# Running five of eight experts over gathered token rows in the last mixture of a twelve-stage decoder kernel

## The chip, the cores and the metric

The kernel runs on one core of a Trainium2 chip. The metric is the device time of one execution in microseconds (us). The program is one launch; its stages follow each other with a barrier of all engines between them.

## The reference

`x` is (8 batches, 128 tokens, 128 features), so 1024 tokens in all. Four layers follow, each an attention, a cross attention and a feed-forward part, always as `x = x + part(layernorm(x))`. The change concerns the last part, a mixture of eight experts with two experts a token and a capacity of 320 places an expert:

```python
cap = floor(2 * 1.25 * 1024 / 8)             # 320
logits = xt @ w_g                            # (1024, 8)
top_v, top_i = top_k(logits, 2)
probs = softmax(logits with all but the two at -inf)
exp_mask = one_hot(top_i, 8) by choice       # first choices of all tokens, then second choices
exp_rank = cumsum(exp_mask over 2 * 1024) - 1
exp_mask = exp_mask * (exp_rank < cap)       # a token whose rank is 320 or more is dropped by that expert
exp_batches = tokens of each expert, 320 rows each
h = gelu(exp_batches @ c_fc)                 # 128 -> 512 for each expert
exp_out = h @ c_proj                         # 512 -> 128
out = sum over the two choices of prob * the token's row of exp_out
```

## The kernel before

All arithmetic is float32. The residual `x_res` lies in SBUF as 128 token rows by 8 batches by 128 features; `xn` is its layer norm, `xnT` the same turned so that features are on partitions and the 1024 tokens are columns.

The last stage is `layer_l3_ffn`, which calls `mixture`. Every expert is run over all 1024 tokens, in two halves of 512 columns: 8 experts x 2 halves = 16 units. A unit is an `up` step on TensorE (four matmuls L1016, each 128 hidden features by 512 tokens, into banks 0 to 3), four gelu activations on ScalarE (L1055) into `hT`, a `down` step on TensorE (16 matmuls L1026: four groups of 128 tokens, each summed over four blocks of hidden features, into one of banks 4 to 6), and four VectorE instructions (L1074) that add the result, scaled by the token's gate for this expert (zero where the expert wasn't chosen or the token was dropped), to `x_res`. The order on TensorE is written out: `up(u)`, then `down(u - 1)`.

Ahead of the units, the layer norm (VectorE L413 to L425, one POOL instruction for each half, L439), eight turns on TensorE (L445) and the router's eight matmuls (L888) run. The routing itself, `RouteWithCapacity.dve`, is a chain of small VectorE instructions in which each waits for the one before (`Link`). It ends with `picked`; TensorE then counts ranks with four small matmuls (`pe_counts`, L931 and L933), which stand behind `up(2)` in its order; VectorE then drops ranks of 320 and more (L962) and makes the gates.

SyncE (SP) loads the weights of each expert (L994, L995; 256 KB each), two experts ahead. POOL does nothing in this stage but the two norm instructions, and no DMA is issued from POOL anywhere in this kernel. Behind the stage comes the block "finish": SP stores `x_res` to `out` and waits for it.

The functions that the diff touches, and what calls them:

## Time and profile before

| | us |
|---|---|
| median of 3 runs (lowest, highest) | 1444.35 (1442.29, 1446.95) |
| the profiled execution, its own time | 1439.21 |
| its span, first to last instruction | 1437.4 |
| TensorE busy in the span | 1257.7 |
| VectorE busy | 698.8 |
| ScalarE busy | 527.4 |
| POOL busy | 393.8 |

The rows below come from the profiled execution. A line such as L1026 is a line of the kernel's file. "PE" is TensorE's matmuls, "PEld" its weight loads, "DVE" VectorE, "ACT" ScalarE, "SPq" SP's queue. One float32 matmul of the program stands in the trace as two records, so x32 of L1026 (or x8 of L1016) is one unit's step. The end of a matmul is modelled in the trace; the pace of TensorE is therefore read from the distance between starts, or from the chain that ended last.

### The profile page before, as it was taken

How to read it: one execution, taken by the hardware profiler on the slowest of the kernel's cores; microseconds unless marked ns; L12 is line 12 of the kernel's file. 1: busy time of each engine (PE TensorE's matmuls, PEld its weight loads, DVE VectorE, ACT ScalarE, POOL GpSimd, SP SyncE). 2: the span in 40 equal slices, each digit the busy share in tenths (PEclk: the TensorE clock that was granted, in tenths of full speed). 3: DMA queues.
4: the chain of work that ended last, by engine and by line, in shares of the span. 5: the costliest groups of instructions: out<-in, count | busy, mean ns of one | idle time of the engine just before them, and what ended most of it. 6: DMA issues, size and time to landing. Idle time of an engine off the chain costs nothing. (4 is left out here: it accounts for less than half of the span.)

```text
span 1437.4 us, 26031 instructions
## 1 busy us (share of the span) xinstructions
PE 1257.7 (87%) x10476; PEld 929.3 (65%) x10476; DVE 698.8 (49%) x2173; ACT 527.4 (37%) x1183; POOL 393.8 (27%) x459
## 2 busy tenths in 40 slices
PE   7999697999866766987887999999899999987998
PEld 5867585788623433664664887785567774565776
DVE  5554533444499245764674226527732137655111
ACT  5533242443355323453443212314433324333332
POOL 7959120000423226744662300002000010040000
PEclk9999798999956678998999559999989989988999
DMA  4000503321380000000000000000021100000010
GB/s 138 1 4 1 190 1 103 89 65 26 118 226 1 1 32 0 1 1 1 1 1 8 2 2 1 1 4 1 9 87 39 36 14 1 4 0 30 30 45 30
DMA packets 46695, 48.42 MB, mean 34 GB/s; under 512 B 18960, under 2 KB 37904, under 8 KB 45552
## 3 DMA queue, kind: packets, MB, share of 16 engines
q1 hardware_dynamic: 46576, 46.76, 10.4%
q8 instruction: 84, 1.38, 0.4%
q14 instruction: 35, 0.29, 0.1%
HBM read 41.91 MB, written 4.85 MB: 33 GB/s over the span
## 5 line engine op out<-in xcount | busy, mean ns | idle before, releaser
L1026 PEld LDWEIGHTS bank<-scratch 128*128 128x128 f32 x1024 | 119.0, 192 | 13.9 <-issue 13.9
L1055 ACT ACTIVATE scratch<-bank 128x512 f32<-128x512 f32 x128 | 76.4, 597 | 135.2 <-PE bank L1016 135.2
L1026 PE MATMUL bank<-scratch 128*128 128x128 f32 x1024 | 119.2, 275 | 0.0
L1016 PE MATMUL bank<-xnT,scratch 128*128 128x512 f32 x256 | 118.7, 609 | 0.0
L1074 DVE SCALAR_TENSOR_TENSOR x_res<-bank,scratch,x_res 128x128 f32<-128x128 f32 x128 | 36.0, 345 | 168.0 <-PE bank L1026 168.0
L615 ACT ACTIVATE scratch<-bank 128x512 f32<-128x512 f32 x96 | 52.5, 594 | 91.7 <-PE bank L516 91.7
L574 DVE TENSOR_REDUCE scratch<-bank 128x4 f32<-128x512 f32 x96 | 63.2, 686 | 38.2 <-PE bank L2180 22.4
L1016 PEld LDWEIGHTS bank<-xnT,scratch 128*128 128x128 f32 x256 | 47.9, 197 | 49.1 <-issue 49.1
L439 POOL TENSOR_TENSOR ln_rstd<-ln_ve,ln_half 128x4 f32<-128x4 f32 x28 | 28.6, 1024 | 178.2 <-DVE ln_ve L418 178.1
L2432 POOL TENSOR_TENSOR scratch<-scratch 128x16 f32<-128x16 f32 x16 | 51.7, 3231 | 52.2 <-DVE scratch L2773 52.2
L580 DVE TENSOR_TENSOR scratch<-bank,scratch 128x512 f32<-128x512 f32 x96 | 61.5, 682 | 0.0
L516 PEld LDWEIGHTS bank<-ident,scratch 128*128 128x128 f32 x384 | 43.9, 146 | 23.9 <-DVE scratch L580 17.0
L516 PE MATMUL bank<-ident,scratch 128*128 128x128 f32 x384 | 54.9, 288 | 4.7 <-DVE scratch L580 4.7
L2170 PE MATMUL bank<-weights 32*128 32x32 f32 x1024 | 54.6, 395 | 2.5 <-DVE scratch L2284 2.5
L2170 PEld LDWEIGHTS bank<-weights 32*128 32x128 f32 x1024 | 54.5, 327 | 3.3 <-issue 3.3
L500 PE MATMUL bank<-scratch 32*128 32x512 f32 x192 | 55.2, 656 | 1.4 <-ACT scratch L2253 1.4
L2461 PE MATMUL bank<-weights,xnT 128*128 128x512 f32 x64 | 40.0, 721 | 14.4 <-DVE scratch L2743 13.8
L2135 POOL TENSOR_TENSOR weights<-weights 128x128 f32<-128x128 f32 x8 | 3.7, 457 | 154.3 <-DVE weights L2314 154.3
L2975 POOL TENSOR_TENSOR scratch<-scratch 128x1024 f32<-128x1024 f32 (+5 forms) x48 | 42.9, 893 | 3.8
L445 PE MATMUL bank<-ident,xn 128*128 128x128 f32 x88 | 21.4, 381 | 23.9 <-DVE xn L425 23.8
L1598 POOL TENSOR_TENSOR x_res<-x_res,scratch 128x256 f32<-128x256 f32 x4 | 2.9, 724 | 142.8 <-ACT scratch L1742 142.8
L2970 POOL TENSOR_TENSOR scratch<-scratch 128x2048 f32<-128x2048 f32 x8 | 36.2, 4525 | 19.7 <-DVE weights L1311 19.3
(527 smaller groups left out, 2835.3 us busy)
## 6 DMA issues: line engine op xcount, KB each, us to landing
scratch<-conv_kernels SPq DMA_DIRECT2D x8, 1024.0 KB, 11.2
scratch<-e_l_ffn_w SPq DMA_DIRECT2D x32, 256.0 KB, 2.9
scratch<-e_l_ffn_w SPq DMA_DIRECT2D x4, 1024.0 KB, 14.5
values<-scratch SPq DMA_DIRECT2D x8, 512.0 KB, 2.7
scratch<-values SPq DMA_DIRECT2D x8, 512.0 KB, 4.2
weights<-w_l_ffn SPq DMA_DIRECT2D x1, 3698.0 KB, 12.2
weights<-w_l_attn SPq DMA_DIRECT2D x1, 2560.5 KB, 9.0
weights<-w_l_attn SPq DMA_DIRECT2D x2, 1024.0 KB, 7.1
```

The source lines that it names most:

```text
L500: s = self.nc.tensor.matmul(self.by_head(self.core.ps[n % 4][:, :]), self.qT[rows, b * P:(b + 1) * P], self.km[rows, :, b * P:(b + 1) * P] ...
L516: t = self.nc.tensor.transpose(self.core.ps[4 + n % 2][:, i * P:(i + 1) * P], self.shift[:, n % 4, i * P:(i + 1) * P], self.core.ident[:, :])
L574: self.nc.vector.tensor_reduce(self.top[:, n % 4, :], self.by_head(self.core.ps[n % 4][:, :]), AX_X, ALU.max, negate=True).then_inc(self.t ...
L580: self.nc.vector.tensor_tensor(self.by_head(self.shift[:, n % 4, :]), self.by_head(self.core.ps[n % 4][:, :]), self.top[:, n % 4, :].unsqu ...
L615: self.nc.scalar.activation(self.prob_of(n), self.by_head(self.core.ps[4 + n % 2][:, :]), ACT.Exp, scale=scale) \
L1016: nc.tensor.matmul(ps[UP_BANKS[i]][:, :], wa[e % 2][:, i * P:(i + 1) * P], core.xnT[:, half(h)], start=True, stop=True).then_inc(up_made.s ...
L1026: mm = nc.tensor.matmul(ps[Y_BANKS[u % 3]][:, t * P:(t + 1) * P], hT[h][:, i, t * P:(t + 1) * P], wb[e % 2][:, i, :], start=(i == 0), stop ...
L1055: nc.scalar.activation(hT[u % 2][:, i, :], ps[UP_BANKS[i]][:, :], act_func) \
L2170: m = nc.tensor.matmul(ps[4 * (r % 2) + j][:, 32 * t:32 * t + 32].rearrange("p (i b) -> p i b", i=4), relk[rows, P - 1 - q:2 * P - 1 - q], ...
L2432: nc.gpsimd.tensor_tensor(rn, ss, power, ALU.pow).then_inc(rooted.sem, rooted.up())
L2461: nc.tensor.matmul(ps[QK_BANKS[n]][:, :], core.xnT[:, b * P:(b + 1) * P], wqkv[d][:, n * BANK:(n + 1) * BANK], start=True, stop=True).then ...
L2975: link(tt(out, prod[:, :, 0:h], prod[:, :, h:2 * h], ALU.add))
```

## The change

`layer_l3_ffn` gets a program of its own in place of `mixture`. Experts 0, 1 and 7 are run as before over all tokens in halves (jobs 0 to 3 and 9, 10). Experts 2 to 6 (jobs 4 to 8) are run over 320 columns each. Their token rows are brought together through DRAM:

- The router also computes for each token and choice a row number (`places`): a row of 1600 (5 x 320) if the choice is one of the five experts and not dropped, else an unused row behind them. The counting matmuls now stand behind `down(0)`. The gate normalization, which stood ahead of `picked`, now stands behind it.
- POOL writes the rows of `xn` to DRAM (`rows_of_tokens`) with 16 indirect DMAs, one for each batch and choice, 128 rows of 512 bytes each. When all 16 have landed, SP reads the 1600 rows back in four DMAs as 13 tiles of 128 rows; TensorE turns them (13 transposes in four groups), VectorE copies each group to `takenT`.
- Each of the five jobs is an `up` of four matmuls over 320 columns, four gelus over 320, a `down` of 12 matmuls, two VectorE copies to `made`, and two DMAs of SP into DRAM (`rows_of_experts`).
- When all ten of those have landed, POOL reads each token's row back with 16 indirect DMAs into `back`, and VectorE adds them with their gates to `x_res` in four groups (16 instructions, L1350), behind the additions of expert 7.
- All experts' weights are loaded at the start of the stage, 4 MB in eight DMAs. At the start of the kernel POOL clears a tile of zeros and SP writes it over the 13 tiles of `rows_of_tokens`.

```diff
-class RouteWithCapacity(Route):
+class RouteToPlaces(Route):
...
+    FIRST, LAST = 2, 7
+    ROWS = (LAST - FIRST) * CAP
...
-        dve.wait_ge(self.exped.sem, self.exped.at(0))
-        link(nc.vector.tensor_tensor(prob, prob, second, ALU.mult))
-        link(nc.vector.tensor_reduce(self.total, prob, AX_X, ALU.add))
-        link(nc.vector.reciprocal(self.total, self.total))
-        link(nc.vector.tensor_tensor(prob, prob, over_experts(self.total), ALU.mult))
...
         v.then_inc(self.picked.sem, self.picked.up())
+        dve.wait_ge(self.exped.sem, self.exped.at(0))
+        link(nc.vector.tensor_tensor(val, first, second, ALU.add))
+        link(nc.vector.tensor_tensor(prob, prob, val, ALU.mult))
+        link(nc.vector.tensor_reduce(self.total, prob, AX_X, ALU.add))
+        link(nc.vector.reciprocal(self.total, self.total))
+        link(nc.vector.tensor_tensor(prob, prob, over_experts(self.total), ALU.mult))
         dve.wait_ge(self.counted.sem, self.counted.at(0))
+        counts = self.by_choice(self.core.ps[self.BANK_OF_SCORES][:, 0:2 * B * 8])
+        link(nc.vector.scalar_tensor_tensor(out=both, in0=counts, scalar=self.CAP + 0.5, in1=both, op0=ALU.is_lt,
+                                            op1=ALU.mult))
+        link(nc.vector.tensor_tensor(self.spots, counts[:, :, some], self.first_row, ALU.add))
+        link(nc.vector.tensor_tensor(self.spots, self.spots, both[:, :, some], ALU.mult))
+        link(nc.vector.tensor_reduce(self.row, self.spots, AX_X, ALU.add))
+        link(nc.vector.tensor_tensor(self.row, self.row, self.unread, ALU.add))
+        nc.vector.tensor_copy(self.core.places[:, :], self.row).then_inc(self.placed.sem, self.placed.up())
...
+    def dve_sources(self, dve):
+        nc, both = self.nc, self.both
+        some = slice(self.FIRST, self.LAST)
+        link = self.link
+        link(nc.vector.tensor_scalar(self.core.sources[:, :], self.row, self.ROWS - 1.0, None, ALU.min))
...
-    mixture(core, tag, c, w1, w2, ACT.Gelu, RouteWithCapacity(core, tag, c, w))
+    route = RouteToPlaces(core, tag, c, w)
+    CAP, FIRST, LAST, ROWS = route.CAP, route.FIRST, route.LAST, route.ROWS
+    dense = lambda experts: [(e, h) for e in experts for h in range(2)]
+    jobs = dense(range(FIRST)) + [(e, None) for e in range(FIRST, LAST)] + dense(range(LAST, E))
+    A, Z = 2 * FIRST, 2 * FIRST + LAST - FIRST
+    COUNTS_AT = 1
...
+            for e in range(2):
+                sp.dma_start(wa[:, e, :], w1[e]).then_inc(loads[e].sem, loads[e].up(16))
+                sp.dma_start(flat(wb[:, e]), w2[e]).then_inc(loads[e].sem, loads[e].up(16))
+            for rest in (slice(2, 5), slice(5, 8)):
+                sp.dma_start(wa[:, rest, :], w1[rest].rearrange("e p f -> p e f")) \
+                    .then_inc(loads[2].sem, loads[2].up(16))
+                sp.dma_start(wb[:, rest].rearrange("p e c d -> p e (c d)"), w2[rest].rearrange("e p f -> p e f")) \
+                    .then_inc(loads[2].sem, loads[2].up(16))
+            sp.wait_ge(put.sem, put.at(2 * B - 1, 16))
+            for g, tiles in enumerate(groups):
+                sp.dma_start(taken[:, tiles, :], core.taken_dram[tiles.start * P:tiles.stop * P, :]
+                             .rearrange("(t p) d -> p t d", p=P)).then_inc(fetched[g].sem, fetched[g].up(16))
+            for j in range(A, Z):
+                s = j - A
+                sp.wait_ge(added.sem, added.at(j))
+                sp.dma_start(core.made_dram[s * CAP:s * CAP + 2 * P, :].rearrange("(t p) d -> p t d", p=P),
+                             made[s][:, 0:2, :]).then_inc(stored.sem, stored.up(16))
+                sp.dma_start(core.made_dram[s * CAP + 2 * P:s * CAP + CAP, :], made[s][0:CAP - 2 * P, 2, :]) \
+                    .then_inc(stored.sem, stored.up(16))
...
+            pool.wait_ge(core.taken_cleared, 16)
+            pool.wait_ge(norm.xn.sem, norm.batch(norm.xn, B - 1))
+            pool.wait_ge(route.placed.sem, route.placed.at(0))
+            for b in range(B):
+                for k in range(2):
+                    n = B * k + b
+                    nc.gpsimd.indirect_dma_start(core.taken_dram, bass.IndirectOffsetOnAxis(core.places[:, n:n + 1], 0),
+                                                 core.xn[:, b, :], None).then_inc(put.sem, put.up(16))
+            pool.wait_ge(route.sourced.sem, route.sourced.at(0))
+            pool.wait_ge(stored.sem, stored.at(2 * (LAST - FIRST) - 1, 16))
+            for b in range(B):
+                for k in range(2):
+                    n = B * k + b
+                    nc.gpsimd.indirect_dma_start(back[:, n, :], None, core.made_dram,
+                                                 bass.IndirectOffsetOnAxis(core.sources[:, n:n + 1], 0)) \
+                        .then_inc(returned[b // 2].sem, returned[b // 2].up(16))
...
+            def up(j):
+                e, h = jobs[j]
+                pe.wait_ge(load_of(e).sem, load_of(e).at(0, 32) if e < 2 else load_of(e).at(0, 64))
+                tokens = takenT[:, (e - FIRST) * CAP:(e - FIRST) * CAP + CAP] if h is None else core.xnT[:, half(h)]
+                for i in range(HC):
+                    if j > 0:
+                        pe.wait_ge(up_out.sem, up_out.at((j - 1) * HC + i))
+                    nc.tensor.matmul(ps[UP_BANKS[i]][:, 0:N(j)], wa[:, e, i * P:(i + 1) * P], tokens,
+                                     start=True, stop=True).then_inc(up_made.sem, up_made.up())
+
+            def down(j):
+                e, h = jobs[j]
+                pe.wait_ge(up_out.sem, up_out.at(j * HC + HC - 1))
+                if j >= 3:
+                    pe.wait_ge(added.sem, added.at(j - 3))
+                for t in range(0, N(j), P):
+                    n = min(P, N(j) - t)
+                    for i in range(HC):
+                        mm = nc.tensor.matmul(ps[Y_BANKS[j % 3]][0:n, t:t + P], hT[j % 2][:, i, t:t + n], wb[:, e, i, :],
+                                              start=(i == 0), stop=(i == HC - 1))
+                mm.then_inc(down_made.sem, down_made.up())
+
+            def turn(g):
+                pe.wait_ge(fetched[g].sem, fetched[g].at(0, 16))
+                if g == 0:
+                    pe.wait_ge(route.done.sem, route.done.at(0))
+                else:
+                    pe.wait_ge(emptied.sem, emptied.at(g - 1))
+                for t in range(groups[g].start, groups[g].stop):
+                    m = nc.tensor.transpose(ps[TURN_BANK][:, t % 4 * P:(t % 4 + 1) * P], taken[:, t, :], core.ident[:, :])
+                m.then_inc(filled.sem, filled.up())
+
+            for h in range(2):
+                norm.pe(pe, h, Y_BANKS[h])
+            pe.wait_ge(*core.w_loaded[tag])
+            pe.wait_ge(x_out.sem, x_out.at(1))
+            route.pe(pe)
+            for j in range(A):
+                up(j)
+                if j > 0:
+                    down(j - 1)
+                if j == COUNTS_AT:
+                    route.pe_counts(pe)
+            down(A - 1)
+            turn(0)
+            for j in range(A, len(jobs) + 1):
+                if j < Z:
+                    pe.wait_ge(emptied.sem, emptied.at(min(j - A, 3)))
+                if j < len(jobs):
+                    up(j)
+                if j - A < 3:
+                    turn(j - A + 1)
+                if j > A:
+                    down(j - 1)
...
+            def add(j):
+                e, h = jobs[j]
+                dve.wait_ge(down_made.sem, down_made.at(j))
+                bank = ps[Y_BANKS[j % 3]]
+                if h is None:
+                    s = j - A
+                    n = CAP - 2 * P
+                    nc.vector.tensor_copy(flat(made[s][:, 0:2, :]), bank[:, 0:2 * P])
+                    v = nc.vector.tensor_copy(made[s][0:n, 2, :], bank[0:n, 2 * P:3 * P])
...
+            def empty(g):
+                dve.wait_ge(filled.sem, filled.at(g))
+                n = (groups[g].stop - groups[g].start) * P
+                nc.vector.tensor_copy(takenT[:, 4 * P * g:4 * P * g + n], ps[TURN_BANK][:, 0:n]) \
+                    .then_inc(emptied.sem, emptied.up())
+
+            def take_back(g):
+                dve.wait_ge(returned[g].sem, returned[g].at(0, 64))
+                for k in range(2):
+                    if k == 1:
+                        dve.wait_ge(summed.sem, summed.at(g))
+                    for b in (2 * g, 2 * g + 1):
+                        n = B * k + b
+                        v = nc.vector.scalar_tensor_tensor(out=x[:, b, :], in0=back[:, n, :],
+                                                           scalar=route.given[:, n:n + 1], in1=x[:, b, :],
+                                                           op0=ALU.mult, op1=ALU.add)
+                    if k == 0:
+                        v.then_inc(summed.sem, summed.up())
...
+            route.dve(dve)
+            dve.wait_ge(route.done.sem, route.done.at(0))
+            for j in range(A):
+                add(j)
+            route.dve_sources(dve)
+            for g in range(3):
+                empty(g)
+            for j in range(A, Z):
+                add(j)
+                if j == A:
+                    empty(3)
+            for j in range(Z, len(jobs)):
+                add(j)
+            dve.wait_ge(added.sem, added.at(len(jobs) - 1))
+            dve.wait_ge(route.sourced.sem, route.sourced.at(0))
+            for g in range(4):
+                take_back(g)
...
+                sp.wait_ge(zeros_made, 1)
+                n = -(-RouteToPlaces.ROWS // P)
+                sp.dma_start(core.taken_dram[0:n * P, :].rearrange("(t p) d -> p t d", p=P),
+                             core.zeros[:, :].unsqueeze(1).broadcast_to([P, n, D])).then_inc(core.taken_cleared, 16)
...
+                nc.gpsimd.memset(core.zeros[:, :], 0.0).then_inc(zeros_made, 1)
```

What stands on TensorE at the front of the stage, before: from the first `up` on. `bank`, `scratch` and `weights` are PSUM banks and SBUF buffers; `scratch` holds expert weights and `hT`.

```order
L1016 MATMUL bank<-xnT,scratch 128x512 [waits expert_weights0]
L1016 MATMUL bank<-xnT,scratch 128x512 x3
L1016 MATMUL bank<-xnT,scratch 128x512 [waits expert_act] x4
L1026 MATMUL bank<-scratch 128x128 [waits expert_act]
L1026 MATMUL bank<-scratch 128x128 x15
L1016 MATMUL bank<-xnT,scratch 128x512 [waits expert_act,expert_weights1]
L1016 MATMUL bank<-xnT,scratch 128x512 [waits expert_act] x3
L931 MATMUL bank<-scratch,weights 128x64 [waits route_picks]
L933 MATMUL bank<-scratch,ones 128x64
```

In the changed kernel TensorE has at this place, from the `down` of job 0 on:

```order
L1263 MATMUL bank<-scratch 128x128 [waits expert_act]
L1263 MATMUL bank<-scratch 128x128 x15
L949 MATMUL bank<-scratch,weights 128x64 [waits route_picks]
L951 MATMUL bank<-scratch,ones 128x64
L949 MATMUL bank<-scratch,weights 128x64
L951 MATMUL bank<-scratch,ones 128x64
L1252 MATMUL bank<-xnT,scratch 128x512 [waits expert_act,expert_weights1]
L1252 MATMUL bank<-xnT,scratch 128x512 [waits expert_act] x3
```

The counts have moved ahead of the third `up`. Further on, TensorE goes in the changed kernel from the dense jobs to those over 320 columns, from the `down` of job 3 on:

```order
L1263 MATMUL bank<-scratch 128x128 [waits expert_added,expert_act]
L1263 MATMUL bank<-scratch 128x128 x15
L1274 MATMUL bank<-ident,scratch 128x128 [waits route_by_token,rows_fetched0]
L1274 MATMUL bank<-ident,scratch 128x128 x3
L1252 MATMUL bank<-scratch 128x320 [waits expert_act,rows_loaded,bank_emptied]
L1252 MATMUL bank<-scratch 128x320 [waits expert_act] x3
L1274 MATMUL bank<-ident,scratch 128x128 [waits bank_emptied,rows_fetched1]
L1274 MATMUL bank<-ident,scratch 128x128 x3
```

Before, the next unit's `up` over 512 columns of `xnT` stands at this place. Behind the `down` of job 3 there are now transposes that wait for `rows_fetched0`; the `up` of job 4 waits for the copy out of their bank, and the next transposes wait for the same copy and `rows_fetched1`.

POOL's end before, with the last two rows of the stage ahead and the whole of its last stage:

```order
L1852 TENSOR_TENSOR scratch<-scratch 128x8 [waits made_clamped] x2
L1838 UNCONDITIONAL_BRANCH
L997 UNCONDITIONAL_BRANCH [waits barrier_Pool_Activation_PE_DVE_SP_gather]
L439 TENSOR_TENSOR ln_rstd<-ln_ve,ln_half 128x4 [waits norm_eps] x2
L986 UNCONDITIONAL_BRANCH
```

In the changed kernel POOL has:

```order
L1221 UNCONDITIONAL_BRANCH [waits barrier_Pool_Activation_PE_DVE_SP_gather]
L439 TENSOR_TENSOR ln_rstd<-ln_ve,ln_half 128x4 [waits norm_eps] x2
L1231 DMA rows_of_tokens<-xn,places 3648x128 [waits route_chosen,norm_xn,rows_cleared]
L1231 DMA rows_of_tokens<-xn,places 3648x128 x15
L1238 DMA scratch<-rows_of_experts,sources 128x128 [waits rows_stored,route_gates]
L1238 DMA scratch<-rows_of_experts,sources 128x128 x15
L1197 UNCONDITIONAL_BRANCH
```

Behind the norm instructions there are now 32 DMAs; the first 16 wait for the row numbers, the second 16 for all stores of the five experts' results.

VectorE's end of the stage in the changed kernel, from the additions of expert 7 on (before, the additions of the last unit, L1074, are its last rows):

```order
L1332 SCALAR_TENSOR_TENSOR x_res<-bank,scratch,x_res 128x128 [waits expert_down]
L1332 SCALAR_TENSOR_TENSOR x_res<-bank,scratch,x_res 128x128 x3
L1350 SCALAR_TENSOR_TENSOR x_res<-scratch,x_res 128x128 [waits rows_returned0,route_gates,expert_added]
L1350 SCALAR_TENSOR_TENSOR x_res<-scratch,x_res 128x128
L1350 SCALAR_TENSOR_TENSOR x_res<-scratch,x_res 128x128 [waits rows_summed]
L1350 SCALAR_TENSOR_TENSOR x_res<-scratch,x_res 128x128
L1350 SCALAR_TENSOR_TENSOR x_res<-scratch,x_res 128x128 [waits rows_returned1]
```

Behind the two units of expert 7, VectorE now waits four times for rows that POOL's DMAs bring back (the groups for `rows_returned2` and `rows_returned3` are not shown).

## Rows read from the trace of the kernel before

**Rows 1.** The page: span, busy time by engine, and the gelu group.

```profile
span 1437.4 us, 26031 instructions
...
PE 1257.7 (87%) x10476; PEld 929.3 (65%) x10476; DVE 698.8 (49%) x2173; ACT 527.4 (37%) x1183; POOL 393.8 (27%) x459
...
L1055 ACT ACTIVATE scratch<-bank 128x512 f32<-128x512 f32 x128 | 76.4, 597 | 135.2 <-PE bank L1016 135.2
```

**Rows 2.** The chain in order of time, last stage: start us, us, what.

```profile
1317.63 8.49 PE bank L1016 x16
1326.12 3.57 PE bank L1026 x32
1329.69 3.44 PE bank L1016 x8
...
1333.96 3.63 PE bank L1026 x32
1337.59 3.44 PE bank L1016 x8
...
1425.10 7.16 PE bank L1026 x64
```

**Rows 3.** Windows: us, busy time of each engine, PEclk, DMA share, GB/s.

```profile
1307.70:1317.60 9.90, 6.01 (x25) 5.01 (x25) 5.36 (x27) 0.79 (x2) 2.04 (x2) 0.50 0.32 108
1317.60:1326.10 8.50, 8.50 (x19) 3.80 (x19) 7.41 (x69) 5.81 (x10) 0.00 (x0) 0.83 0.00 0
...
1340.20:1432.30 92.10, 92.05 (x546) 68.43 (x544) 14.66 (x53) 29.85 (x50) 0.00 (x0) 1.00 0.09 30
```

**Rows 4.** Timeline of VectorE from 1300 us: start, us, group, idle before.

```profile
1302.91 0.42 DVE L2063 TENSOR_TENSOR x_res<-x_res,bank 128x256 f32<-128x256 f32 x1 [1.20 <-PE bank L1948]
...
1327.10 1.37 DVE L956 TENSOR_TENSOR scratch<-scratch 128x8 f32<-128x8 f32 x7
1334.00 0.48 DVE L962 SCALAR_TENSOR_TENSOR scratch<-bank,scratch 128x64 f32<-128x64 f32 x2 [5.53 <-PE bank L933]
...
1334.77 0.28 DVE L965 TENSOR_TENSOR scratch<-scratch 128x64 f32<-128x64 f32 x1
...
1337.62 1.13 DVE L1074 SCALAR_TENSOR_TENSOR x_res<-bank,scratch,x_res 128x128 f32<-128x128 f32 x4 [1.42 <-PE bank L1026]
```

**Rows 5.** Timeline of TensorE in an earlier stage, matmuls of 264 columns.

```profile
200.84 1.95 PE L1235 MATMUL bank<-scratch 128*128 128x264 f32 x8
202.63 1.94 PE L1254 MATMUL bank<-scratch 128*128 128x264 f32 x8
```

**Rows 6.** Timeline of the end of the kernel.

```profile
1432.28 1.12 DVE L1074 SCALAR_TENSOR_TENSOR x_res<-bank,scratch,x_res 128x128 f32<-128x128 f32 x4 [2.45 <-PE bank L1026]
1433.76 0.39 SPq L3633 DMA_DIRECT2D out<-x_res  x1
```

**Rows 7.** Groups of VectorE instructions: busy us, mean ns of one.

```profile
L1063 DVE COPY xnT<-bank 128x512 f32<-128x512 f32 x2 | 1.4, 691 | 1.1 <-PE bank L445 1.1
```

**Rows 8.** Groups of POOL instructions, whole kernel, by shape.

```profile
L2432 POOL TENSOR_TENSOR scratch<-scratch 128x16 f32<-128x16 f32 x16 | 51.7, 3231 | 52.2 <-DVE scratch L2773 52.2
...
L439 POOL TENSOR_TENSOR ln_rstd<-ln_ve,ln_half 128x4 f32<-128x4 f32 x28 | 28.6, 1024 | 178.2 <-DVE ln_ve L418 178.1
```

**Rows 9.** The page's DMA issues: KB each, us to landing.

```profile
scratch<-e_l_ffn_w SPq DMA_DIRECT2D x4, 1024.0 KB, 14.5
values<-scratch SPq DMA_DIRECT2D x8, 512.0 KB, 2.7
```

**Rows 10.** DMA issues from 1307 us on, KB each, us to landing.

```profile
scratch<-e_l_ffn_w SPq DMA_DIRECT2D x16, 256.0 KB, 2.9
```

**Rows 11.** Timeline of SP's queue, 5 to 160 us.

```profile
7.75 1.41 SPq L3569 DMA_DIRECT2D weights<-w_l_xattn  x1
88.15 0.33 SPq L3569 DMA_DIRECT2D weights<-w_l_ffn  x1
```

**Rows 12.** Timeline of SP's queue at the start of the last stage.

```profile
1308.60 0.43 SPq L994 DMA_DIRECT2D scratch<-e_l_ffn_w  x1
```

97 lines of the change are left out of this document (88 added, 9 removed).

## The prediction

> **What bounds the kernel now.** I read the page first, for who is busy: TensorE, 1257.7 of the span's 1437.4 us [rows 1]. Then the chain in order of time, for the stage that is changed: from 1317.63 us it holds nothing but TensorE, `up` at 3.44 us (the first two, which the chain makes one piece, 8.49) and `down` at about 3.57, up to 1432.26, where the last piece ends (1425.10 + 7.16) [rows 2]. The windows say the same: 92.05 of 92.10 us busy, at a granted clock of 1.00 [rows 3]. VectorE's last addition ends at 1433.4, and `out` is issued at 1433.76 [rows 6]. So in this stage every microsecond taken from TensorE shows, until something else is later. Gelu takes 597 ns for 512 columns [rows 1], four of them 2.4 us of a unit's 7.0: ScalarE has room. POOL is free.
>
> **What TensorE is spared.** An expert over all tokens costs two units, 2 x (3.44 + 3.57) = 14.0 us [rows 2]. Over 320 columns an `up` is four matmuls. One of 512 columns takes 3.44 / 4 = 0.86 us, one of 264 takes 1.79 / 4 = 0.448 (starts at 200.84 and 202.63; x8 records are four matmuls) [rows 5]. Both are about 1.7 ns a column, so 320 columns are 0.54 us and the `up` 2.15. The `down` is 12 of the old 16 matmuls, 2.68. Together 4.83 us, 9.2 less; for five experts 45.9. The 13 transposes are matmuls of 128 columns like those of `down`, 0.223 each, 2.9 in all. Net: 43.0 us less TensorE work. Gelu over 320 columns, at most 0.6 us each, stays below TensorE's 4.83 a job.
>
> **The front: when the rows are back.** The counts now follow `down(0)`, which ends at 1329.69, and take 0.83 (1333.96 - 3.44 - 1329.69) [rows 2]: 1330.5. They need `picked`, which was there by 1328.5 even with the gate steps ahead of it [rows 4]. The six VectorE steps to `places` cost 0.26 each (four steps in 1334.00 to 1335.05) [rows 4]: 1332.1. POOL then issues 16 indirect DMAs at c us each. The last lands some 2.7 us behind its issue (the nearest write to DRAM, `values`) [rows 9], and SP's read takes 2.9 (a load of 256 KB) [rows 10]. First rows back: 1332.1 + 16c + 5.6 = 1337.7 + 16c.
>
> TensorE comes to `turn(0)` at 1330.5 + 2 x 3.44 + 3 x 3.57 = 1348.1. From the rows on it does, up to the end of `down(8)`: 13 transposes 2.9, five `up` and five `down` 24.15, the `up` of job 9 3.44; and twice it stands for VectorE's copy out of the transposes' one bank, 0.69 [rows 7] and 0.1 around it, 1.6. Sum 32.1. While it stands waiting, its clock may go: ahead of this stage it was busy for 6.01 of 9.90 us at a granted 0.50 (the 1.2 GHz level), and the first two `up` took 8.49 instead of 6.88 [rows 2, 3]. I charge those 1.6 once more. `down(8)` ends at 1337.7 + 16c + 33.7 = 1371.4 + 16c.
>
> Behind the waiting instructions: on SP the four reads stand behind the wait for all 16 writes, and the stores of results behind the reads, but the first result comes 8 us after the rows, so no store is held. On VectorE three copies out of the transposes' bank stand ahead of the first result's copy; TensorE's own order has them first too. On POOL nothing else waits.
>
> **The end: when the results are back.** VectorE copies the last expert's result, 0.42 for 256 columns [rows 4] and about 0.25 for the rest; SP issues two stores, the second 0.4 later, and it lands 2.7 on: 3.8 us. POOL then issues 16 reads, 16c; the last lands after 2.9; VectorE adds four slices, 1.4 at most (1.13 for four from a bank [rows 4]). Together 8.1 + 16c behind `down(8)`. TensorE meanwhile has 3.57 + 3.44 + 3.57 = 10.6 us of expert 7 and VectorE 1.1 behind it: 11.7 us of cover, the rest of 16c is bare. End: 1379.5 + 32c, against 1433.4 now.
>
> **So the gain is 53.9 - 32c**, and c decides. No DMA is issued from POOL before, so c has to be bounded. Below: an issue from SP, 0.39 us [rows 6]; there the front's wait vanishes (rows back at 1343.9, before 1348.1), and the gain is 39. Above: each transfer is done before the next begins, 2.7 to 2.9 us [rows 9, 10], a loss of 32 to 39. Between: POOL's instruction on 128x4 elements takes 1.02 [rows 8], and SP's longest issue into an empty queue 1.41 [rows 11]. An indirect DMA has 128 rows to look up and to describe, so I set it between these two, at 1.2. Then 16c is 19.2: rows back at 1356.9, TensorE stands 8.8 us; `down(8)` ends at 1390.6, the stage at 1417.9; the bare wait at the end is 15.6. Check: 43.0 - 8.8 - 1.6 - 1.6 - 15.6 = 15.4. Gain 15.5 us.
>
> The Trainium skill, page "DMA: Bandwidth & Descriptors", section "Anatomy of one DMA", fits a DMA from POOL at about 2.0 us and its bytes over 436 GB/s; for 64 KB that is 2.15. An estimate by that page with 2.15 as the pace of the 16 gives 53.9 - 68.8, a loss of 14.9, or 1459. The same section lays most of the 2 us to the write's receipt, which a following DMA need not wait for; no row here shows either. Of rival (2) below I give 0.10 to this rule.
>
> **Costed at nothing.** The clearing at the start: SP's issue stands ahead of the load of `w_l_xattn`, issued at 7.75, whose user starts at 88.15, when the next load is issued [rows 11]; 80 us cover it. POOL's memset is one more of a start that waits for nothing of POOL's. The expert loads: 4 MB at once landed in 14.5 us in another mixture [rows 9], the first expert's parts stand first in the queue, and the five experts are needed 30 us later. If that cover failed, TensorE would start later by a few us. `dve_sources` and the first three groups of returned rows lie under waits for POOL.
>
> **Rivals.** (1) POOL issues fast, c from 0.39 to 0.9: gain 39 to 25, 1405 to 1419 us. For it: SP issues in 0.4. Against: POOL builds descriptors in software and all its rows of this size are slow. Chance 0.15. (2) The other side: POOL's pace is over 1.68 us (53.9 / 32), because its transfers don't overlap, or by the look-up of 128 indices (a POOL instruction on 128x16 elements takes 3.23 us [rows 8]). At 2.1 the time is 1458, at 2.9 it is 1483. For it: no row shows POOL's DMAs overlapping. Against: SP's do, its loads are issued 0.4 us apart and land in 2.9 [rows 10, 12]. Chance 0.24. (3) The change does on TensorE what it says but gives it all back: c from 1.55 to 1.82, within 4.3 us of before. Chance 0.06. (4) The forecast, c from 0.9 to 1.55: gain 25 to 4.3. Chance 0.55.
>
> **The numbers.** The profiled execution took 1439.21, so it would take 1423.7. The median of the three runs is 1444.35, 5.1 above it; less 15.5 it is 1428.9. About 0.3%, 4.3 us, is what a measurement of this kernel can tell from no change. Faster: (4) and (1), 0.70. Same: 0.06. Slower: 0.24. The range leaves out c under about 0.6 (gain 35, 1409) and over about 2.1 (loss 13, 1458). The likeliest case's own range is 1419 to 1440.
>
> **What would show it.** POOL's issues stand c = 1.2 us apart. The `down` of job 3 ends near 1348, an idle stretch of 9 us on TensorE follows, then transposes and jobs of 4.8 us; expert 7's last matmul near 1401, then 15 us in which only POOL and the DMA queues work, VectorE ending near 1418. The prediction is wrong if c is far from 1.2, if landings from POOL take much longer than 2.7 and 2.9, or if TensorE stays at the 0.50 clock well behind its wait.

## The result, and the profile after

The changed kernel takes 1431.82 us, the median of four runs (1424.39 to 1433.34), against 1445.21 for the kernel before on the same chip (1442.29 to 1446.95): a ratio of 0.9901, 95% interval 0.9882 to 0.9920. So it is faster, by 13.4 us where 15.5 were forecast. The profiled execution took 1433.34 us, with a span of 1431.5.

The page of the changed kernel, beside [rows 1]:

```profile
span 1431.5 us, 25584 instructions
...
PE 1223.0 (85%) x10249; PEld 901.8 (63%) x10249; DVE 699.1 (49%) x2172; ACT 512.5 (36%) x1163; POOL 424.7 (30%) x492
...
q0 software_dynamic: 1024, 2.10, 0.7%
```

TensorE does 34.7 us less and POOL 30.9 us more. A queue that did not exist before, q0, carries POOL's transfers: 2.10 MB in 1024 packets, with only 0.7% of the DMA engines' time. Bytes are not what these transfers cost.

TensorE in the timeline of the changed kernel, from the fourth `up` on (L1252 is `up`, L1263 `down`, L1274 the transposes):

```profile
1344.19 3.60 PE L1252 MATMUL bank<-xnT,scratch 128*128 128x512 f32 x8
1347.63 7.31 PE L1263 MATMUL bank<-scratch 128*128 128x128 f32 x64
1364.21 1.11 PE L1274 MATMUL bank<-ident,scratch 128*128 128x128 f32 x4 [9.27 <-DMA scratch<-rows_of_tokens]
1366.10 4.64 PE L1252 MATMUL bank<-scratch 128*128 128x320 f32 x8 [0.78 <-DVE scratch L1340]
1370.53 1.06 PE L1274 MATMUL bank<-ident,scratch 128*128 128x128 f32 x4
1372.38 2.42 PE L1252 MATMUL bank<-scratch 128*128 128x320 f32 x8 [0.78 <-DVE scratch L1340]
...
1383.23 2.42 PE L1252 MATMUL bank<-scratch 128*128 128x320 f32 x8
1385.49 2.96 PE L1263 MATMUL bank<-scratch 128*128 128x128 f32 x24
1388.39 2.42 PE L1252 MATMUL bank<-scratch 128*128 128x320 f32 x8
...
1403.51 7.31 PE L1263 MATMUL bank<-scratch 128*128 128x128 f32 x64
```

The reader is to see the idle stretch of 9.27 us in front of `turn(0)`, released by the read of the gathered rows; then two `up` over 320 columns with 0.78 us of waiting ahead of each, the first of them taking 4.64 us and the second 2.42; and that the last matmul ends at 1410.8, long before the stage does. POOL over the same time, its first two and last writes, its first and last reads:

```profile
1339.85 1.26 POOL L1231 DMA_INDIRECT rows_of_tokens<-xn,places  x1 [21.52 <-DVE places L988]
1341.41 0.97 POOL L1231 DMA_INDIRECT rows_of_tokens<-xn,places  x1 [0.30 <-issue]
...
1359.11 0.96 POOL L1231 DMA_INDIRECT rows_of_tokens<-xn,places  x1 [0.30 <-issue]
1403.71 0.98 POOL L1238 DMA_INDIRECT scratch<-rows_of_experts,sources  x1 [43.64 <-DMA rows_of_experts<-scratch]
...
1422.50 0.94 POOL L1238 DMA_INDIRECT scratch<-rows_of_experts,sources  x1 [0.30 <-issue]
```

A write is issued every 1.26 us, 0.96 of busy time and a gap of 0.30 called issue, for which the profile shows no cause; a read every 1.25 ((1422.50 - 1403.71) / 15). The windows of the changed kernel, in the columns of [rows 3]:

```profile
1355.00:1364.20 9.20, 0.00 (x0) 0.00 (x0) 1.88 (x8) 0.00 (x0) 3.85 (x5) 0.66 0.29 87
1364.20:1372.30 8.10, 6.60 (x16) 4.13 (x16) 1.36 (x2) 1.75 (x4) 0.00 (x0) 0.54 0.17 47
1372.30:1400.00 27.70, 27.62 (x166) 21.65 (x166) 3.46 (x11) 9.38 (x20) 0.00 (x0) 1.00 0.09 25
...
1410.70:1427.30 16.60, 0.12 (x2) 0.00 (x0) 6.04 (x20) 0.00 (x0) 9.69 (x11) 0.66 0.29 45
```

Of these the third is the only one in which TensorE works as it did before; in the last, 16.6 us long, only POOL, VectorE and the DMA engines work. The chain in order of time ends with it:

```profile
1400.72 0.37 SPq L1216
...
1401.13 1.79 DMA rows_of_experts<-scratch
...
1403.71 0.98 POOL scratch L1238
1404.69 0.30 issue
...
1422.50 3.45 DMA scratch<-rows_of_experts,sources
```

After the store of the last expert's result, the chain is nothing but POOL's issues until the last read lands. The last stage took 126.0 us before (1307.76, the first piece of its chain, to the issue of `out` at 1433.76 [rows 6]) and takes 113.3 now (1314.56 to 1427.87), 12.7 less. It begins 6.8 us later than before. The eleven stages ahead of it drift by some us from execution to execution: in the kernels below the last stage begins at 1309.6 to 1318.4. So where two profiled executions are compared, the length of the last stage is given too, from its first layer norm to the issue of `out`: 126.0 before, 113.3 in the changed kernel.

### The profile page after: what moved, and what is told of

It reads as the page before. It is cut to its first block and busy times, and to the rows that moved or that the text cites. A ratio compares the mean times of both kernels' runs of the same rounds, so it can differ in the third digit from the quotient of the medians.

```text
span 1431.5 us, 25584 instructions
## 1 busy us (share of the span) xinstructions
PE 1223.0 (85%) x10249; PEld 901.8 (63%) x10249; DVE 699.1 (49%) x2172; ACT 512.5 (36%) x1163; POOL 424.7 (30%) x492
## 3 DMA queue, kind: packets, MB, share of 16 engines
q0 software_dynamic: 1024, 2.10, 0.7%
## 5 line engine op out<-in xcount | busy, mean ns | idle before, releaser
L615 ACT ACTIVATE scratch<-bank 128x512 f32<-128x512 f32 x96 | 52.6, 594 | 93.1 <-PE bank L516 93.1
L1061 PEld LDWEIGHTS bank<-scratch 128*128 128x128 f32 x512 | 59.5, 192 | 7.2 <-issue 7.2
L1090 ACT ACTIVATE scratch<-bank 128x512 f32<-128x512 f32 x64 | 38.2, 597 | 67.3 <-PE bank L1051 67.3
L1109 DVE SCALAR_TENSOR_TENSOR x_res<-bank,scratch,x_res 128x128 f32<-128x128 f32 x64 | 18.0, 344 | 87.5 <-PE bank L1061 87.5
L1061 PE MATMUL bank<-scratch 128*128 128x128 f32 x512 | 59.6, 275 | 0.0
L1051 PE MATMUL bank<-xnT,scratch 128*128 128x512 f32 x128 | 59.5, 610 | 0.0
L1312 ACT ACTIVATE scratch<-bank 128x512 f32<-128x512 f32 (+1 forms) x44 | 23.1, 524 | 54.6 <-PE bank L1252 53.6
L3216 POOL TENSOR_TENSOR scratch<-scratch 128x2048 f32<-128x2048 f32 x8 | 36.2, 4520 | 19.7 <-DVE weights L1557 19.3
```

Source lines behind the costliest of these rows:

```text
L615: self.nc.scalar.activation(self.prob_of(n), self.by_head(self.core.ps[4 + n % 2][:, :]), ACT.Exp, scale=scale) \
L1051: nc.tensor.matmul(ps[UP_BANKS[i]][:, :], wa[e % 2][:, i * P:(i + 1) * P], core.xnT[:, half(h)], start=True, stop=True).then_inc(up_made.s ...
L1061: mm = nc.tensor.matmul(ps[Y_BANKS[u % 3]][:, t * P:(t + 1) * P], hT[h][:, i, t * P:(t + 1) * P], wb[e % 2][:, i, :], start=(i == 0), stop ...
L1090: nc.scalar.activation(hT[u % 2][:, i, :], ps[UP_BANKS[i]][:, :], act_func) \
```

## The experiments

Each ratio is to the kernel before on the same chip. The kernels ran on several chips, on which the kernel before took 1442.2 to 1445.2 us, so a difference of two medians from different chips is uncertain by some us. Each diff shows the lines that matter; what is left out stands as `...`. Where an edit says "four experts" or "three experts", the constant and its bounds are changed:

```diff
-    FIRST, LAST = 2, 7
+    FIRST, LAST = 2, 6
```

**The price of POOL's return.** The 16 indirect reads are replaced by eight plain ones of SP:

```diff
-            for b in range(B):
-                for k in range(2):
-                    nc.gpsimd.indirect_dma_start(back[:, n, :], None, core.made_dram, ...)
+            ...
+            for g in range(4):
+                for k in range(2):
+                    ...
+                    sp.dma_start(back[:, n:n + 2, :], core.made_dram[0:2 * P, :].rearrange("(t p) d -> p t d", p=P))
```

> Leaves out POOL's 16 indirect reads: eight plain DMAs of SP read the same number of bytes from fixed rows in their place (so the rows added are not those of the tokens). Theory (POOL's issue pace sets the bare wait at the end): the rows are back by about 7 us behind the last store, under expert 7's matmuls; what stays bare is VectorE's 16 additions, about 5 us. The stage ends about 10 us earlier than in the changed kernel: 1421 us, ratio to before about 0.983. Rival (the wait at the end is the latency of transfers, which plain DMAs have too): under 3 us of change. Rival (TensorE is the bound to the end): no change.

Measured: 1420.21 us (1415.92 to 1422.92), ratio 0.9833 (0.9811 to 0.9856). That is 11.6 us below the changed kernel by the medians, 9.8 by the two ratios (0.9901 - 0.9833, of 1443), and the last stage is 10.6 shorter (102.7). The end in VectorE's timeline of this kernel, the second half of expert 7 and the returned rows:

```profile
1411.15 1.13 DVE L1330 SCALAR_TENSOR_TENSOR x_res<-bank,scratch,x_res 128x128 f32<-128x128 f32 x4 [2.45 <-PE bank L1261]
1412.31 4.79 DVE L1348 SCALAR_TENSOR_TENSOR x_res<-scratch,x_res 128x128 f32<-128x128 f32 x16
```

The four waits for returned rows are gone, but the 16 additions, which lay under those waits, now stand bare in one piece of 4.79 us: the next in line behind POOL is VectorE.

**The price of POOL's fill.** The same for the 16 writes, replaced by two of SP:

```diff
-                    nc.gpsimd.indirect_dma_start(core.taken_dram, ..., core.xn[:, b, :], None)
+            ...
+            for h in range(2):
+                sp.dma_start(core.taken_dram[h * 1024:h * 1024 + 1024, :].rearrange("(t p) d -> p t d", p=P), core.xn[:, :, :])
```

> Leaves out POOL's 16 indirect writes: SP writes xn to DRAM by two plain DMAs of the same rows, so the five experts get rows in plain order. Theory: TensorE's idle stretch of 9.3 us ahead of the transposes goes wholly, and with it the slow transposes and the slow first 320-column step behind it (granted clock down during the wait), 2 to 2.5 us more: about 12 us less than the changed kernel, 1420 us, ratio about 0.982. Rival (the slow steps behind the wait have another cause, the first read of takenT say): 9.3 us only, and the first step stays at 4.4 us. Rival (latency of the transfers and not POOL's pace sets the wait): the idle stretch stays over 5 us.

Measured: 1424.35 us (1418.36 to 1426.05), ratio 0.9864 (0.9833 to 0.9895). Below the changed kernel that is 7.5 us by the medians, 5.3 by the ratios and 9.4 by the last stage (103.9), less than the 12 expected. TensorE's timeline of this kernel, with what it waits for:

```profile
1354.28 0.60 PE L1272 MATMUL bank<-ident,scratch 128*128 128x128 f32 x4
1357.08 4.11 PE L1250 MATMUL bank<-scratch 128*128 128x320 f32 x8 [2.20 <-DVE scratch L1338]
```

The idle stretch is gone, and 2.20 us of waiting for VectorE's copy take a part of its place: VectorE has the last additions of expert 1 and the sources ahead of that copy. And the first `up` over 320 columns still takes 4.11 us. A window over it (1357.00:1361.00) shows a granted clock of 0.57, and the changed kernel's window over the transposes and this step one of 0.54 (1364.20:1372.30, above): most of this step ran at the 1.2 GHz level, here behind 2.20 us of waiting.

**Both prices together.** Both edits at once:

> The changed kernel with both of POOL's parts replaced by plain transfers from SP's queue: two writes of all normalized rows in place of the 16 indirect writes, and eight reads of 256 fixed rows in place of the 16 indirect reads. The places' rows and what comes back are other tokens' rows, so the output isn't the reference's; the work of TensorE, ScalarE and VectorE is that of the changed kernel. It is the floor of the change without POOL's pace. If the two terms of the sum are independent, it is the changed kernel's 1431.8 less 11.6 (plain return) less 7.5 (plain fill) = 1412.7, ratio 0.978. Rival: the front's gain is partly taken back by VectorE, which copies the transposed rows only after the third expert's sums and the sources, and the end is bound by VectorE's 16 additions in either case: then more than 1416.

Measured: 1412.88 us (1412.18 to 1416.27), ratio 0.9786 (0.9750 to 0.9822). Its last stage takes 93.1 us, 20.2 less than the changed kernel's, and the two prices taken the same way, 10.6 and 9.4, add up to 20.0. By the medians it is 18.9 (11.6 + 7.5 = 19.1), by the ratios 16.6 (9.8 + 5.3 = 15.1). So the two terms are independent as far as these measurements tell, and POOL's indirect DMAs take 17 to 20 us from this change.

**Four experts on places.** Expert 6 goes back to all tokens, so that it lies over the return:

> Four experts over their places instead of five (2 to 5); expert 6 goes over all tokens beside expert 7 at the end. Computes the same output. Theory: TensorE does 8.2 us more, but the wait of 15.5 us at the end, which no work covers, has 14 us more cover and all but goes: the stage is 5 to 6 us shorter than in the changed kernel, 1426 us, ratio about 0.9865. Rival (each expert taken off the full path is worth its TensorE time): 8 to 9 us slower than the changed kernel, ratio about 0.996.

Measured: 1441.61 us (1433.27 to 1445.59), ratio 0.9988 (0.9966 to 1.0010). The theory missed by 15.6 us; the last stage takes 120.9 us, 7.6 more than the changed kernel's instead of 5 to 6 less. TensorE's timeline of this kernel over the last `down` steps:

```profile
1406.96 1.95 PE L1263 MATMUL bank<-scratch 128*128 128x128 f32 x16
1409.09 0.27 PE L1263 MATMUL bank<-scratch 128*128 128x128 f32 x1 [0.18 <-issue]
1411.19 0.50 PE L1263 MATMUL bank<-scratch 128*128 128x128 f32 x3 [1.83 <-issue]
1412.62 0.27 PE L1263 MATMUL bank<-scratch 128*128 128x128 f32 x1 [0.93 <-issue]
1414.03 0.65 PE L1263 MATMUL bank<-scratch 128*128 128x128 f32 x2 [1.14 <-issue]
...
1416.85 6.96 PE L1263 MATMUL bank<-scratch 128*128 128x128 f32 x40 [0.35 <-issue]
```

These 64 records are the two `down` of expert 7 (the expectations below speak of expert 6 in this place). They should stand in one piece of 7.31 us, as in the last row of the changed kernel. Instead, after 16 of them, they come singly or by two and three, and the pieces' starts are 0.70 us apart or a multiple of it (1.43 from 1411.19 to 1412.62, 0.73 from 1416.12 to 1416.85): eight records take 7.8 us, where 0.9 is normal. Every gap is called "issue": TensorE waits for nothing that the profile shows. The crawl begins 14.6 us after POOL's first read (1394.26) and ends 3.8 us after the last is issued (1413.04). The two windows around it:

```profile
1408.90:1416.80 7.90, 2.08 (x9) 1.25 (x7) 1.13 (x4) 0.00 (x0) 3.86 (x5) 0.84 0.26 46
1416.80:1423.80 7.00, 6.81 (x40) 6.36 (x40) 1.13 (x4) 2.06 (x4) 0.00 (x0) 0.70 0.01 4
```

2.08 of 7.90 us are busy, and behind it the granted clock is 0.70 for a while. The last matmul ends at 1423.8 instead of 1414.3 (1406.96 + 7.31): 9.5 us, some 7 of them the crawl and most of the rest the clock behind it (40 records in 6.96 us instead of 4.6). On top of that VectorE's 16 additions stand bare (4.79 us, as with the plain return).

**The clearing, moved.** SP's DMA of zeros is issued ahead of `l1_ffn` instead of at the start:

```diff
-                sp.wait_ge(zeros_made, 1)
-                ...
-                sp.dma_start(core.taken_dram[0:n * P, :]...)          # at the start
+            if name == "l1_ffn":
+                ...
+                nc.sync.dma_start(core.taken_dram[0:tiles * P, :]...)
```

> The DMA that clears rows_of_tokens is issued ahead of the sixth stage instead of in the start block. Theory: its issue occupies SP for 4.2 us from 4.95 us on and holds the barrier behind the start block for 1.5 to 1.9 us; moved, the first layer norm begins at 8.2 us as before and the kernel is 1 to 2 us shorter than the changed one, ratio about 0.989. My prediction's step (hidden at nothing): no change anywhere.

Measured: 1432.76 us (1421.25 to 1435.33), ratio 0.9912 (0.9883 to 0.9942), the changed kernel's time within the measurement (the last stage is 113.2 us). But the start shows what it did. SP's queue in the changed kernel's timeline:

```profile
4.95 4.22 SPq L3841 DMA_DIRECT2D rows_of_tokens<-zeros  x1
9.65 4.42 SPq L3824 DMA_DIRECT2D weights<-w_l_xattn  x1
```

And the same load, and the zeros, in the timeline of the kernel with the late clearing:

```profile
7.91 1.20 SPq L3824 DMA_DIRECT2D weights<-w_l_xattn  x1
...
533.97 0.43 SPq L3882 DMA_DIRECT2D rows_of_tokens<-zeros  x1
```

At the start the issue of the zeros (1664 rows) holds SP for 4.22 us, and the next load is issued at 9.65 instead of 7.91. The one after it comes at 89.08 against 88.36: 0.7 us stay, too little to measure. Moved to 533.97, the issue of the same DMA takes 0.43 us: it was long for where it stood, behind eight loads issued in the 4.2 us before it, and not for its 1664 rows.

**What makes POOL slow, and what makes TensorE crawl.** With four experts, half the bytes in each write and half the rows in each read:

```diff
-    indirect_dma_start(core.taken_dram, ...places[:, n:n + 1]..., core.xn[:, b, :], None)
+    indirect_dma_start(core.taken_dram.rearrange("r (h d) -> (r h) d", h=2), ..., core.xn[:, b, 0:64], None)
-    indirect_dma_start(back[:, n, :], None, core.made_dram, ...sources[:, n:n + 1]...)
+    indirect_dma_start(back[0:64, n, :], None, core.made_dram, ...sources[0:64, n:n + 1]...)
```

> Experts 2 to 5 on places (expert 6 over all tokens at the end, as in the run with four experts), and the 16 writes of the fill carry 256 bytes for each of 128 rows instead of 512, the 16 reads of the return fetch 64 rows each instead of 128, of 512 bytes. Rows 64 to 127 of what comes back are left out, and half of each row of the fill, so the output isn't the reference's; every engine's own work is that of the run with four experts. Two questions. (1) What does POOL's 1.26 us pace count? By the instruction: writes and reads stay at 1.26 and 1.25 us apart. By the index (one descriptor for each): writes at 1.26, reads at 0.65 to 0.8. By the byte: both at 0.65 to 0.8. (2) What makes TensorE crawl at 0.70 us for each matmul in the second half of a burst? Theory A, a queue of descriptors that fills (descriptors written faster than the DMA engines take them away): with half the descriptors the return never gets there, no crawl over expert 6's jobs, the last stage ends some 8 us earlier than in the run with four experts (span near 1428 against 1435.9); the crawl in the fill stays. Rival B, so many instructions of the kind (after the 11th): the crawl over expert 6 stays, after the 11th read. Rival C, bytes under way: the crawl goes in both.

Measured: one run, 1445.33 us. POOL's timeline of this kernel, two writes and two reads:

```profile
1345.15 0.97 POOL L1231 DMA_INDIRECT rows_of_tokens<-xn,places  x1 [0.30 <-issue]
1346.43 0.96 POOL L1231 DMA_INDIRECT rows_of_tokens<-xn,places  x1 [0.30 <-issue]
...
1403.96 0.92 POOL L1239 DMA_INDIRECT scratch<-rows_of_experts,sources  x1 [0.30 <-issue]
1405.19 0.90 POOL L1239 DMA_INDIRECT scratch<-rows_of_experts,sources  x1 [0.30 <-issue]
```

The writes keep their 1.26 us with half the bytes; the reads go from 1.25 to 1.21 ((1420.87 - 1402.73) / 15) with half the rows. So the pace counts instructions, and 64 rows fewer save 0.04 us. The crawl came again in both bursts, 13.9 us after the first write and 14.3 after the first read, so it goes neither by bytes nor, in the return, by the number of rows described: this expectation's theories A and C fall.

**A pause in the burst.** Four experts, and POOL waits until its first eight have landed:

```diff
+                if b == 3:
+                    pool.wait_ge(put.sem, put.at(7, 16))
```

> The run with four experts, with one change: POOL waits for its first 8 indirect writes to land before it issues the other 8, and the same between the first 8 and the last 8 reads. Nothing is left out of the computation. Each pause costs POOL some 1.5 to 3 us (a landing of 2.2 in the fill, 3.0 in the return, less the issue that was to come anyway). Theory A (TensorE crawls when a burst of POOL's indirect transfers is longer than some 11 of them without a break): no matmul 0.70 us apart over expert 6's jobs, which gives back 8 us at the end; the fill's pause stands on the path in front of turn(0) and costs 1.5 to 2.5. Sum: 1441.6 - 8 + 2 = about 1435.5, ratio 0.994. Rival B (the crawl comes from a time since the first such transfer, or from how many there were in all): it comes again at the same matmuls, and the time is 1441.6 + 2 = 1443.5, ratio 1.001.

Measured: 1435.37 us (1433.45 to 1440.05), ratio 0.9940 (0.9919 to 0.9962), as the theory of this expectation had it: 6.2 us less by the medians than the same kernel without pauses, and 5.3 less in the last stage (115.6). In TensorE's timeline the last piece is whole again:

```profile
1411.11 7.31 PE L1268 MATMUL bank<-scratch 128*128 128x128 f32 x64
```

**A wait that costs no time.** The same place, but for something that has long been there:

```diff
+                if b == 3:
+                    pool.wait_ge(core.taken_cleared, 16)              # fill
+                    pool.wait_ge(returned[0].sem, returned[0].at(0, 64))  # return
```

> The run with four experts, where POOL waits in front of its ninth write and of its ninth read for something that has long been there (the clearing of the buffer; the first four reads' landing, over 2 us before). Nothing is left out of the computation. It asks what ended TensorE's crawl in the run with a pause: that POOL stood idle for 1.5 and 2.8 us there, or that the row of 16 like instructions was broken by a wait at all. Theory (POOL must stand idle, or what it has issued must have landed): the pace stays 1.26 and 1.25 without a gap, and the crawl comes again as in the run with four experts, after some 11 transfers, costing 7 to 8 us over expert 6's jobs (span near 1436). Rival (the row of like instructions counts): no crawl, span near 1428.

Measured: one run, 1431.78 us, 9.8 below the median with four experts and below the lowest of its ten runs; the last stage takes 111.4 us, 9.5 less than with four experts. POOL's timeline in this kernel, the eighth and the ninth read:

```profile
1408.27 0.95 POOL L1240 DMA_INDIRECT scratch<-rows_of_experts,sources  x1 [0.30 <-issue]
1409.52 0.95 POOL L1240 DMA_INDIRECT scratch<-rows_of_experts,sources  x1 [0.30 <-issue]
```

TensorE's last piece in its timeline:

```profile
1412.33 7.31 PE L1267 MATMUL bank<-scratch 128*128 128x128 f32 x64
```

No gap on POOL, and no crawl. I had expected the opposite; the rival came true. It is one execution, and it ran on another chip than the kernels that crawl; more on that at the end.

**Three experts on places** (3 to 5), so that expert 2 lies over the fill:

```diff
-    FIRST, LAST = 2, 7
+    FIRST, LAST = 3, 6
```

> Experts 3 to 5 on places; 0, 1, 2 and 6, 7 over all tokens. Nothing is left out of the computation. Against the run with four experts TensorE does one expert more over all tokens, 8.6 us more by the sum of the prediction (43.0 for five), and that work lies beside POOL's fill: the wait of 9.3 us for the rows in front of turn(0) goes, and with it the slow first step behind it (2.3). Theory A (a long burst of POOL's indirect transfers slows TensorE wherever it stands): expert 2's matmuls now lie under the late part of the fill and crawl for about 8 us, and expert 6's under the late part of the return as before: 1441.6 + 8.6 - 11.6 + 8 = 1446.6, ratio 1.003. Rival B (the crawl belongs to the end of the kernel, or to what runs there): the front is clean, 1441.6 + 8.6 - 11.6 = 1438.6, ratio 0.997.

Measured: 1445.63 us (1439.63 to 1448.74), ratio 1.0002 (0.9982 to 1.0022). Theory A: both bursts show the crawl, the fill over expert 2 and the return over expert 7 (TensorE's last two `down` begin at 1420.77 and end at 1436.5, 15.7 us instead of 7.3). The gaps in the fill's crawl begin 16.8 us after the first write, later than elsewhere. The first and the last piece of the return's crawl in TensorE's timeline of this kernel:

```profile
1420.77 1.39 PE L1263 MATMUL bank<-scratch 128*128 128x128 f32 x11
...
1429.56 6.94 PE L1263 MATMUL bank<-scratch 128*128 128x128 f32 x46 [0.34 <-issue]
```

**Four experts behind three** (3 to 6 on places, 7 behind), with the fill's pause and the late clearing:

```diff
-    FIRST, LAST = 2, 7
+    FIRST, LAST = 3, 7
```

> Experts 3 to 6 on places, 0 to 2 ahead and 7 behind over all tokens, with the fill's pause and the late clearing. Nothing is left out. Against the changed kernel (experts 2 to 6, 1431.8): one expert more over all tokens, +8.6; it lies beside POOL's fill, so the wait of 9.3 for the rows in front of turn(0) goes, and the slow first step behind it, 2.3; the late clearing, 0.7: 1428.1, ratio 0.988. The end is that of the changed kernel: the return bare for 16 us behind expert 7. Rival: VectorE's and ScalarE's part of expert 2, or a crawl that the pause does not take away in the front, eats the 3 us: 1432 or more.

Measured: 1431.45 us (1428.34 to 1436.15), ratio 0.9922 (0.9895 to 0.9949). No crawl in the fill (in the return TensorE is done 7.1 us after the first read), and no wait for the rows; but the copy behind `turn(0)` makes TensorE wait for 2.17 us instead of 0.78, since VectorE has expert 2's additions and the sources ahead of it, and the `up` behind that takes 4.11 again. Both were counted as gone: 1428.1 + 1.4 + 1.7 (4.11 against 2.42) = 1431.2, near the rival's value and the measured one; this sum was made after the result.

**Three experts, with all that helps.** Pauses, the late clearing, and VectorE's additions of tiles 0 to 5 ahead of the last half:

```diff
-            for j in range(Z, len(jobs)):
-                add(j)
-            for g in range(4):
-                take_back(g)
+            for j in range(Z, len(jobs) - 1):
+                add(j)
+            ...
+            for g in range(3):
+                take_back(g)
+            ...
+            add(len(jobs) - 1)
+            ...
+            take_back(3)
```

> Experts 3 to 5 on places, with four edits at once: both pauses of POOL (after the eighth write and the eighth read, until the first eight have landed); VectorE adds the returned rows of tiles 0 to 5 before the last expert's second half and only those of tiles 6 and 7 behind it; the buffer is cleared in l1_ffn's place in SP's queue instead of at the start. Nothing is left out. From the run with three experts (1445.6): two crawls of 7.5 to 8 us each go (-15.5); TensorE's last matmul then ends before the last rows are back, so of the 3.6 us that VectorE's earlier additions could give some 2 remain; the pause of the fill is hidden under expert 2, that of the return (1.5 to 2.8) is in part bare; the clearing gives 0.7. Sum about 1428.5 to 1430, ratio 0.989. Rival: with the crawls gone POOL's return is the bound as in the changed kernel (last read issued some 2.8 us later than without a pause), so that no more than 10 us come back: 1434 or more.

Measured: 1428.29 us (1422.61 to 1430.37), ratio 0.9899 (0.9847 to 0.9951), as expected; the last stage takes 109.4. The last one replaces the pauses by the waits that cost nothing, and moves VectorE's work further forward:

```diff
+                if j == len(jobs) - 2:
+                    ...
+                    take_back(0)
+                    take_back(1)
+                    ...
+                if j == len(jobs) - 1:
+                    take_back(2)
+                    ...
                 add(j)
+            take_back(3)
```

> Experts 3 to 5 on places, the late clearing, and in place of the two pauses the waits that cost POOL nothing (in front of the ninth write and the ninth read, for what has long been there). VectorE adds the returned rows of tiles 0 to 3 ahead of expert 7's first half, those of tiles 4 and 5 ahead of its second half and those of tiles 6 and 7 last, and makes the sources after it has copied the taken rows (0.8 us in front of them before). Nothing is left out. From the run with three experts and pauses (1428.3): its end waited for the last rows, issued at 1416.65 and added by 1421.3; without the gap of 3.0 the last are issued near 1413.8 and here near 1417, and VectorE's last additions end 1.3 us behind them or behind expert 7's sums (TensorE's end at 1416, plus 1.1 and 1.3): 1418.4, which is 2.9 less. The sources behind the copy give 0.8. Sum 1424.6, ratio 0.987, if no crawl comes. Rival: the crawl comes back in one or both bursts (the one profile without a pause and without a crawl was chance): 1432 to 1440.

Measured: 1422.77 us (1419.81 to 1427.31), ratio 0.9866 (0.9840 to 0.9892). It beats the kernel before by 20.2 us on the same chip, and by the two ratios to the kernel before (0.9866 and 0.9901) it is 5 us below the changed kernel, by the medians 9; the intervals of the two ratios overlap a little. Its last stage takes 104.7 us against 113.3. Its TensorE, from expert 2's last `down` to the first `up` over 320 columns, and at the end:

```profile
1359.83 6.97 PE L1267 MATMUL bank<-scratch 128*128 128x128 f32 x61
1366.64 0.60 PE L1278 MATMUL bank<-ident,scratch 128*128 128x128 f32 x4
1368.62 2.42 PE L1256 MATMUL bank<-scratch 128*128 128x320 f32 x8 [1.38 <-DVE scratch L1344]
...
1406.55 7.31 PE L1267 MATMUL bank<-scratch 128*128 128x128 f32 x64
```

VectorE's end in the timeline of the same kernel:

```profile
1411.42 1.25 DVE L1354 SCALAR_TENSOR_TENSOR x_res<-scratch,x_res 128x128 f32<-128x128 f32 x4
1413.95 1.13 DVE L1336 SCALAR_TENSOR_TENSOR x_res<-bank,scratch,x_res 128x128 f32<-128x128 f32 x4 [1.28 <-issue]
1415.22 1.26 DVE L1354 SCALAR_TENSOR_TENSOR x_res<-scratch,x_res 128x128 f32<-128x128 f32 x4
```

No idle stretch at the front, no crawl in either burst, a first `up` at the full clock, and behind TensorE's last matmul (1413.8) only expert 7's additions and one group of four.

## Why the prediction was right

**The formula** was a gain of 53.9 - 32c for the stage. The measured pace is 1.26 for the fill and 1.25 for the return: c = 1.255 gives 13.7. The stage shortened by 12.7, the medians by 13.4. So c = 1.2 was 0.05 too low, worth 1.8 of the 2.1 us by which the forecast was too good. But 1.2 was set between two other instructions and not read from a row: the sum around c was sound, and that c came so close was luck. The sign rested on c staying below 1.68. Other terms were off by as much and cancel, as follows.

**TensorE's saving.** The page shows 34.7 us less busy time instead of 43.0. Of the difference, 4.4 don't belong to the change: in the eleven stages ahead, the same in both kernels, the matmuls were busy for 1137.0 us before and for 1141.4 in the changed kernel. In the last stage it is 39.1 less (120.7 and 81.6). The jobs over 320 columns take 1.6 more than forecast: they come 5.16 us apart (1383.23 to 1388.39), not 4.83, since an `up` takes 2.26 and a `down` 2.90. The steps at the low clock take 3.2 (below). The 13 transposes take 1.5 less: a transpose stands in the trace as one record of 0.11 us (x4 for four of them), and the prediction charged each as a matmul of `down`, which has two, 0.223. That leaves some 0.6; busy time is by modelled ends.

**The front.** Predicted: rows at 1356.9, and 8.8 us of waiting. Measured: 1364.21 with the stage 6.8 us later, so 0.5 behind the forecast, and 9.27 of waiting. The row numbers were ready when they should be (1338.96 less 6.8 is 1332.2, forecast 1332.1). POOL's first write came 0.9 later, 0.8 of it called issue: a term that the prediction does not have. From there to the first transpose it took 24.4 us and not 24.8: fifteen intervals between the writes, 19.3, then 2.2 to the landing of the last and 2.8 to that of SP's first read, instead of 19.2, 2.7 and 2.9. **The wait for the one bank** was forecast at 1.6 us and is two times 0.78. **The clock** was charged 1.6 us; the first `up` took 4.64 instead of 2.42, and the transposes ahead of it and behind it 1.11 and 1.06 instead of 0.60 (the third group): 3.2 together, twice the charge. The run with the plain fill shows that this doesn't hang on the long wait: after 2.20 us it is there too (4.11), in the last kernel after 1.38 us it is not (2.42). After 2.14 us it was there with three experts and pauses (4.11) and absent with three experts and no pause (2.42). What decides it is left open.

**The end.** Predicted: 15.6 us bare. Measured: TensorE's end at 1410.8, VectorE's at 1427.2, of which 1.1 are expert 7's additions: 15.3. Here the errors cancel too: c was too low, and there are 0.8 us between the last store's landing and POOL's first read that were not counted, but the store landed after 1.8 us instead of 2.7. Taking the reads off POOL shortened the stage by 10.6 us and not by 16, mainly because VectorE's 16 additions, cheap under the waits, then stand bare; that a formula in c alone would end in another bound below some c, the prediction did not say.

**Costed at nothing.** The clearing was not free: I had looked at the use of the load behind it, at 88 us, and not at the length of the issue itself and what else waits for it. The first layer norm, at 8.22 before, begins at 9.68, and at 8.15 with the clearing moved; by 89 us 0.7 of this is left. The expert loads and the sources did cost nothing in the changed kernel.

**Rivals.** Fast POOL (0.15) and slow POOL (0.24) are ruled out by the pace. The Trainium skill's fit in "DMA: Bandwidth & Descriptors", section "Anatomy of one DMA", gave 2.15 us for 64 KB: that is what a write here takes to land (2.2), not what the next one waits for, and the estimate of 1459 built on it as a pace falls. That POOL's transfers overlap is seen in the reads: issued 1.25 apart, they land 3.0 us after their issue (the median).

**What the prediction could not see** is that the changed kernel just escapes the crawl: in the return its TensorE is done 7 us after the first read, and in the fill it has matmuls only until 15.1 us after the first write. In the profiled execution these ran at their full pace; in two kernels of the same order, those with the plain return and with the late clearing, the crawl had begun at 13.6 us, under the wait for the rows, and cost nothing. The splits that cover POOL's bursts of 16 with TensorE's work met it in all six such bursts.
